# Shared image rows of a deformable convolution: copied by ScalarE in place of a transfer

## What is computed

```python
om = conv3x3(x, w_off) + b_off                      # 27 channels: 9 dy, 9 dx, 9 masks
py = off_y + row + ky;  px = off_x + column + kx    # where each of 9 taps looks
sampled = bilinear(x, py, px) * sigmoid(om[:, 18:]) # per tap, pixel and channel
out = einsum('bckhw,ock->bohw', sampled, w) + b
out = relu(batch_norm(out)) + x
```

## Time and profile before

| | |
|---|---|
| median of 3 runs | 800.93 us (799.81 to 804.2) |
| the profiled execution | 804.77 us, of which its span is 803.0 us |
| TensorE busy | 633.6 us (79%) |
| VectorE busy | 585.3 us (73%) |
| ScalarE busy | 523.7 us (65%) |
| GpSimd busy | 511.5 us (64%) |
| transfers of the SP and ACT queues, share of 16 DMA engines | 60.2% |
| `region<-region` transfers (the shared rows) | 31 of 576 KB, 7.0 us from issue to landing |
| `region<-wg` transfers (the weights) | 31 of 72 KB, 7.6 us to landing |

### The profile page before, as it was taken

One profiled execution on the slowest core, in us unless ns is written; L12 is line 12 of the kernel. 1 busy time (PEld: TensorE's weight loads), 2 busy tenths in 40 slices (PEclk: granted clock), 3 DMA queues, 4 the chain that ended last, 5 costly groups with the idle time before them and its releaser, 6 DMA issues.

```text
span 803.0 us, 32829 instructions
## 1 busy us (share of the span) xinstructions
PE 633.6 (79%) x13656; PEld 477.1 (59%) x13656; DVE 585.3 (73%) x782; ACT 523.7 (65%) x838; POOL 511.5 (64%) x469
## 2 busy tenths in 40 slices
PE   5989999985999769889879998678676877777722
PEld 1335666653445557677667777566576766667622
DVE  2477877885322569999878999688979877768845
ACT  2656766674223669797777897477668776767505
POOL 3035444440420468999887999587879877877730
PEclk9999999997999999999989999798989999989967
DMA  4000000000373678999999998887879999998202
GB/s 175 1 0 2 2 0 0 0 1 1 83 180 92 166 201 223 259 253 253 248 231 213 266 253 230 189 213 188 227 176 216 210 217 240 231 212 217 58 2 105
DMA packets 55085, 121.14 MB, mean 151 GB/s; under 512 B 23135, under 2 KB 27231, under 8 KB 54752
## 3 DMA queue, kind: packets, MB, share of 16 engines
q1 hardware_dynamic: 53154, 119.53, 60.2%
q10 hardware_dynamic: 1854, 0.58, 0.3%
HBM read 79.47 MB, written 3.28 MB: 103 GB/s over the span
## 4 chain that ended last, share of the span: by engine, by line
PE 45%; DVE 15%; DMA 11%; issue 9%; SPq 9%; ACT 8%; POOLq 1%; ACTq 0%; POOL 0%; DVEq 0%
PE PS L1338 40%; DMA region<-wg 9%; DVE region L922 8%; SPq L411 4%; DVE region L933 3%; PE PS L1433 3%; ACT region L1184 2%; ACT region L1181 1%; SPq L398 1%; DMA region<-px_scratch 1%; PE PS L1425 1%; PE PS L1424 1%; SPq L405 1%; ACT region L1135 1%; DMA px_scratch<-two 1%
## 5 line engine op out<-in xcount | busy, mean ns | idle before, releaser
L1338 PE MATMUL PS<-region 64*64 64x112 f32 (+5 forms) x12176 | 445.3, 270 | 104.1 <-DVE region L922 35.1
L1338 PEld LDWEIGHTS PS<-region 64*64 64x64 f32 (+2 forms) x12176 | 369.0, 140 | 161.1 <-issue 144.5
L922 DVE TENSOR_TENSOR region<-PS,region 128x1024 f32<-128x1024 f32 (+1 forms) x256 | 298.6, 1203 | 85.5 <-PE PS L1338 81.6
L631 POOL TENSOR_TENSOR region<-region 128x960 f32<-128x960 f32 x128 | 239.4, 1870 | 78.0 <-DVE region L922 77.9
L1184 ACT ACTIVATE region<-region 128x1152 f32<-128x1152 f32 x128 | 149.1, 1165 | 34.7 <-PE PS L1338 23.7
L1181 ACT ACTIVATE region<-region,cst 128x1152 f32<-128x1152 f32 x128 | 159.3, 1245 | 0.9 <-DMA region<-px_scratch 0.9
L634 POOL TENSOR_TENSOR region<-region 128x320 f32<-128x320 f32 x128 | 117.1, 915 | 10.0
L933 DVE TENSOR_REDUCE region<-region 128x32 f32<-128x736 f32 x128 | 116.1, 908 | 0.0
L1200 ACT ACTIVATE region<-PS 128x432 f32<-128x432 f32 (+1 forms) x93 | 44.7, 481 | 86.1 <-PE PS L1338 86.0
L554 POOL TENSOR_TENSOR region<-region,cst 128x512 f32<-128x512 f32 x32 | 33.8, 1056 | 63.3 <-PE PS L1425 58.7
L593 POOL TENSOR_TENSOR region<-x,cst 128x504 f32<-128x504 f32 x32 | 34.3, 1072 | 24.0 <-ACT x L1299 12.1
(11 more groups left out here) (139 smaller groups left out, 636.3 us busy)
## 6 DMA issues: line engine op xcount, KB each, us to landing
region<-px_scratch SPq DMA_DIRECT2D x256, 288.0 KB, 6.3
region<-region SPq DMA_DIRECT2D x31, 576.0 KB, 7.0
region<-xp SPq DMA_DIRECT2D x31, 264.0 KB, 6.4
region<-wg SPq DMA_DIRECT2D x31, 72.0 KB, 7.6
out<-region SPq DMA_DIRECT2D x4, 512.0 KB, 3.0
x<-xp SPq DMA_DIRECT2D x16, 82.5 KB, 4.2
x<-xp SPq DMA_DIRECT2D x16, 82.4 KB, 4.1
x<-xp SPq DMA_DIRECT2D x16, 82.2 KB, 4.3
```

What stands on the lines that cost most here:

```text
L631: pool.tensor_tensor(two_rows[:, :, :, 0:NA - FOLD], two_rows[:, :, :, 0:NA - FOLD], two_rows[:, :, :, FOLD:NA], ALU.add).then_inc(half_re ...
L922: v.tensor_tensor(uu[:, 2 * u:2 * u + 2, :, lo:hi], PS[:, banks:banks + 2, 0:(hi - lo) * C].rearrange("p h (a o) -> p h o a", o=C), awf[:, ...
L1338: return nc.tensor.matmul(o, l, r, start=start, stop=stop)
```

## The change

Three things change. `share_rows(s)` leaves SP's queue and becomes an ACTIVATE with the function Copy in ScalarE's order, in step 2 of chunk s, behind `hats` (and `samples_out`) and ahead of `vertical_hat`; its semaphore `shared` counts by one and replaces `shared_in`. The weights `wgr` are loaded only when a buffer's pair changes: for s = 0, 1, 7, 8, 15, 16, 23 and 24, 8 transfers in place of 31, with a semaphore `wg_in` of their own, for which TensorE waits beside `xr_in`. And `few_in` is dropped; `xs_in[0]` counts on in its place.

```diff
             def copy_rows(s):
...
                 sp.dma_start(xr[s % 2].rearrange("p r c -> p (r c)"), xp[:, a:a + RPC * (W + 2)]).then_inc(xr_in[s % 2], 16)
-                sp.dma_start(wgr[:, s % 2, :], wg[:, (s + 1) // NCH, :]).then_inc(xr_in[s % 2], 16)
+                if s < 2 or (s + 1) % NCH < 2:
+                    sp.dma_start(wgr[:, s % 2, :], wg[:, (s + 1) // NCH, :]).then_inc(wg_in[s % 2], 16)
...
                     load_px(g, c * RPC + line, line, px_in)
                     if line == GR:
-                        share_rows(s)
                         if s + 1 < PAIRS * NCH - 1:
                             copy_rows(s + 1)
-
-            def share_rows(s):
-
-                src, dst = FIRSTS + RPC * (s // NCH), RING + 2 * RPC * ((s + 1) % 2)
-                if s % NCH < NCH - 1:
-                    src = RING + 2 * RPC * (s % 2) + RPC
-                if s >= 1:
-                    sp.wait_ge(row_out, done(3 * s - 1))
-                sp.wait_ge(fi_out, 3 * 4 + 5)
-                sp.wait_ge(t_ready, 3 + 2 * SPC * s)
-                sp.dma_start(imgf[:, dst:dst + RPC, :].rearrange("p r a -> p (r a)"), imgf[:, src:src + RPC, :].rearrange("p r a -> p (r a)")).then_inc(shared_in[s % 2], 16)
...
+            def share_rows(s):
+
+                src, dst = FIRSTS + RPC * (s // NCH), RING + 2 * RPC * ((s + 1) % 2)
+                if s % NCH < NCH - 1:
+                    src = RING + 2 * RPC * (s % 2) + RPC
+                act.wait_ge(row_out, done(3 * s - 1))
+                act.wait_ge(fi_out, 3 * 4 + 5)
+                act.wait_ge(t_ready, 3 + 2 * SPC * s)
+                a.activation(imgf[:, dst:dst + RPC, :], imgf[:, src:src + RPC, :], ACT.Copy).then_inc(shared, 1)
...
                     if i in (1, 3) and not (last and end):
                         b = i // 2
                         act.wait_ge(t_ready, 3 + 2 * SPC * s)
-                        act.wait_ge(shared_in[(s + 1) % 2], 16 * (s // 2 + 1))
+                        act.wait_ge(shared, s + 1)
                         slots_out(3 * s + b, slot + 3 * b, b, slot_bank(s, b))
                     if i == 2 and s < AHEAD and s % 2 == 1:
                         samples_out(NCH + s // 2, 7)
+                    if i == 2 and not (last and end):
+                        share_rows(s)
...
                 if b == 0:
-                    pe.wait_ge(xr_in[e], j * 32 + 32)
+                    pe.wait_ge(xr_in[e], j * 16 + 16)
+                    pe.wait_ge(wg_in[e], (j + e >> 2) * 16 + 16)
                 slot_round(3 * s + b, e, b, bank)
...
                 pe.wait_ge(row_out, done(3 * s - 1))
-                pe.wait_ge(shared_in[1 - e], j * 16 + 16)
+                pe.wait_ge(shared, s + 1)
```

More of the change, by code:

```diff
@@ L298, in build @@
         xs_in = [sem("xs_in%d" % j) for j in range(4)]
-        few_in, shared_in, xr_in = sem("few_in"), [sem("shared_in0"), sem("shared_in1")], [sem("xr_in0"), sem("xr_in1")]
+        shared, xr_in, wg_in = sem("shared"), [sem("xr_in0"), sem("xr_in1")], [sem("wg_in0"), sem("wg_in1")]
         px_stored = [sem("px_stored0"), sem("px_stored1")]
@@ L397, in copy_few @@
                         a = (XPAD - 1 + n * RPC) * (W + 2) + kx
-                        sp.dma_start(xs[32 * kx:32 * (kx + 1), 0:FEW - kx], xp[32 * g:32 * (g + 1), a:a + FEW - kx]).then_inc(few_in, 16)
+                        sp.dma_start(xs[32 * kx:32 * (kx + 1), 0:FEW - kx], xp[32 * g:32 * (g + 1), a:a + FEW - kx]).then_inc(xs_in[0], 16)
             def copy_rows(s):
@@ L424, in _ @@
                     copy_rows(0)
-            sp.sem_inc(shared_in[1], 16)
             def load_next(s):
@@ L1046, in _ @@
             for s, n in ((k_out, 2), (q_staged, 4), (ln_ready, 2), (q_out, 2), (v_out, 2), (exp_ready, 2), (vt_out, 6), (pt_out, 4),
-                         (ye_out, 2), (sg_ready, 2), (row_out, 2), (fi_out, 2), (mk_out, 2), (py_out, 2), (g_im_out, 6), (ab_ready, 2), (wt_ready, 2), (g_ab, 2), (g_wt, 2), (z_ready, 2)):
+                         (ye_out, 2), (sg_ready, 2), (row_out, 2), (fi_out, 2), (mk_out, 2), (py_out, 2), (g_im_out, 6), (ab_ready, 2), (wt_ready, 2), (shared, 1), (g_ab, 2), (g_wt, 2), (z_ready, 2)):
                 act.sem_inc(s, n)
@@ L1605, in between_in_loop @@
                 if u == 0:
-                    pe.wait_ge(few_in, 16 * 6 * (n + 1))
+                    pe.wait_ge(xs_in[0], 16 * 6 * (n + 2))
                     turn(n)
```

## The result

The changed kernel took **769.98 us** (median of 4 runs, 768.94 to 774.97) against 800.37 us for the kernel before in the same comparison: a ratio of **0.9642, 95% interval 0.9563 to 0.9722**. The forecast was 779 with 770 to 793, so the kernel is faster, as forecast, by 30 us and not 22, and the time lies 0.02 us under the low end of the range. The profiled execution took 769.77 us, its span 768.0.

The account below looks back on a forecast made before the run. It took queued DMA transfers to cost time in chunks 2 to 15 and SP's issuing to bound 21 to 27. 12.6 + 11.4 + 0.5 = 24.5 us off 804.77 gave 780.3, or 776.5; it said 779, range 770 to 793.

Parts of the forecast that it names:

- The 12.6: Chunks 2 to 15: gain of 12.6 us, 203.68 less 191.1, from waits for new rows and weights going to nothing.
- the slow stretch around 405 us: Chunks 2 to 15: place where one `wg` landing took 12.46 us; its return would hide part of the gain.
- 13.65: Chunks 2 to 15: the engines' pace in us a chunk; a pair of chunks takes 27.3 us.
- the estimate of 11.6: Chunks 2 to 15: DMA work a chunk of about 11.6 us, from 20% fewer bytes at 14.55 us.
- The term was 11.4: Chunks 21 to 27: gain of 11.4 us from SP's issue time, 107.27 less 95.9; 5 if the stall moves to `xr`.
- the 13.7: Chunks 21 to 27: forecast us a chunk, taken beside SP's round of 13.6, GpSimd's 13.39 and chunk 27's 13.81.
- Here SP itself is the bound: Chunks 21 to 27: claim that SP's issuing sets the pace, its round falling from 15.93 us to 13.6.
- Nothing in it waits for long: Chunks 21 to 27: claim that SP's 15.93 us round of issues and register loads holds no long wait.
- The transfers are not what these stretches wait for: Chunks 16 to 20 (28 to 31 at 0): claim leaving 0.5 us of gain, for the first loop's last `wg` wait.
- the first rival: Both long stretches: ScalarE with the copy takes the pace, less is given back; 786 to 795 us, chance 0.16.
- Hidden anyway (801): Whole kernel: the transfer was already hidden and the engines set the pace; 797 to 805, about 801 us, chance 0.11.
- Slower (807): ScalarE, every chunk: the copy holds back `wt` of step 3, 28 us lost against 24.5 gained; 807 us, chance 0.09.

## Why the prediction was right, and where it was not

**Chunks 2 to 15, right in kind.** The pairs take 27.3 us as forecast (191.66 / 7 = 27.38) and the waits for `wg` there are gone. The 12.6 was read from one execution; by the second profile of the kernel before it is 5.6. That the first comparison shows 12.0 beside it is luck of that execution. The prediction named the slow stretch around 405 us and put the term at 6 for the case that only half of the gain comes: that value was nearer. The DMA share was to fall to about 0.8 and fell to 0.92: bytes fell by 18% (245 GB/s over 203.68 us against 214 over 191.66) and DMA busy time by 13% (203.7 against 176), so the share did not follow the bytes here. What mattered, 12.6 us of DMA work a chunk (0.92 x 13.69) below 13.65, held, by far less than the estimate of 11.6.

**Chunks 21 to 27, near in size, by a step that failed.** The term was 11.4 and measured 7.3. Most of the difference is one wait: chunk 21 took 17.61 us (569.98 to 587.59), and TensorE waited 4.21 us in it with the name "issue". The six chunks behind it took 82.38 us, 13.73 each, where the forecast had 13.7. In the profile of the kernel before, the longest such wait stood in chunk 20, ahead of the stretch from which the term was taken (start, us; the changed kernel first):

```profile
581.19 7.12 PE L1338 MATMUL PS<-region 64*64 64x144 f32 x176 [4.21 <-issue]
```

```profile
587.91 8.01 PE L1338 MATMUL PS<-region 64*64 64x112 f32 x189 [3.15 <-issue]
```

Chunks 20 to 27 together, where the cut does not matter, gave 10.8 us (10.0 by the second profile of the kernel before).

What failed is the way to the 13.7. "Here SP itself is the bound" and "Nothing in it waits for long" took SP's round for a sum of issues, and five times 1.36 us for `wg` as most of the gain. But the weights alone brought 2.0 us in chunks 20 to 27 and nothing in time, the shared rows' removal alone 9.2; the 1.36 became 0.60 when the shared rows left. And SP did wait, for ScalarE's `wt`, and waits longer after the change. SP's waits in chunks 20 to 27, before and after:

```profile
SPq L411 <- ACT region L1184: 10.4, 8, 4.5
```

```profile
SPq L412 <- ACT region L1172: 17.4, 12, 4.2
```

SP's rounds after the change, from `xr` to `xr` from 573.96 us on, are 15.6, 16.1, 14.3, 13.1, 14.2 and 14.1 us, 14.6 on average, against 15.93 and a forecast of 13.6. SP is one part of the circle shown above: two more issues a round gave about half of their time. That six chunks come out at 13.7 is in part luck.

**Chunks 16 to 20 and the ends, the step that was wrong.** "The transfers are not what these stretches wait for" was concluded from a DMA share of 0.78 and 0.59 and from the absence of named waits. They gave 15.0 us with chunks 0 and 1 (by the second profile of before, chunks 0 and 1, 16 to 19 and 28 to 31 give 8.3 of 23.5). In chunks 16 to 19 the time went with waits of the name "issue", 11.1 us before, which are TensorE's waits for instructions, and they went and came back with the transfer. The prediction did not cost that name at all. Chunk 20 gave 3.5 of the 8.0, because the long wait of that name stands in chunk 21 now. For the ends the cause stays open: in chunks 0 and 1 the waits are fewer (9.3 and 4.8) but did not come back with the transfer, and in chunks 28 to 31 they are the same (10.8 and 10.7) and the stretch is 2.5 us shorter all the same.

**The copy, right.** 1156 ns and 1.06 from start to start, against 1.08; hidden in chunks 2 to 15, where leaving it out gave nothing. In chunks 20 to 27, where the forecast had it at 0, leaving it out gave 2.8 to 3.9 us, of which about 0.7 is left without TensorE's "issue" waits; that is as much of the first rival, ScalarE taking the pace, as the runs show.

**The rivals.** Hidden anyway (801): fell. The rule of the Trainium skill that stands beside it (page "DMA: Bandwidth & Descriptors", section "Rules for kernel authors": issue early, compute, wait late) speaks of a transfer's own wait, which was indeed hidden; taking away the transfer alone was still worth 0.9611, and putting one back made others wait (10.4 us for `xr` in chunks 20 to 27 against 4.6). Slower (807): its mechanism exists, but its price was a copy's whole excess in every chunk; at double the copy the loss was 7 us, so most of an excess of 1.05 us a chunk found cover (that this is because ScalarE runs ahead is argued).

**Size.** 24.5 us by its own sum and 30 measured; the spans of the profiles differ by 35.0, and by the second profile of the kernel before by 23.5. The terms missed in both directions: up to 7 us too many in chunks 2 to 15 and 4 in 21 to 27, 8 to 14.5 too few in the others. That the sum came as near as it did is partly luck, because these errors cancel.

## What to carry to other kernels

A transfer for which nobody waits can be the one that costs: look at what lands behind it, and take the named wait as the end of a queue, not as its cause. Where a stretch is a circle through a queue, TensorE and ScalarE, adding up one member's time gives a bound that its members do not reach; a single edit tells less than the edit of each. Profile the kernel before twice ahead of taking a term of 12 us from one stretch of one execution, and look at whether a long wait lies on the same side of the cut before and after.

## What the runs showed of the hardware

- The issue of a transfer on SP's queue can stall behind others: the issue of `wg` took 0.60 to 1.63 us (median 1.28 of 31) behind the 576 KB transfer, and 0.60 in 29 of 31 places once that transfer was gone.
- In chunks whose program is written out, TensorE's waits with no named releaser were 8.1 to 11.1 us in four chunks beside a transfer of 512 or 576 KB a chunk, at a DMA share of 0.75 to 0.85, and 3.6 to 7.2 us without. Each of them ended 1.2 to 1.8 us behind a packet of the instruction queue.
- In chunks 2 to 15 a transfer of 512 KB a chunk at a DMA share of 0.99 cost 1 us of 192: the share alone does not tell whether a transfer costs.
